# Stage 1 of a Mamba and expert-choice layer: TensorE adds the residual rows into the projection's PSUM, ScalarE evacuates, and the slots of all steps are set anew

## The reference, cut to what matters

```python
xz = einsum('bld,ed->ble', x, in_proj_w); x_, z = split(xz, 2)     # 512 + 512 features
u = silu(conv1d(x_) + b)                                           # 4 taps per feature
dt_low, B, C = split(einsum(u, x_proj_w))                          # 16 + 16 + 16
delta = softplus(dt_low @ dt_proj_w.T + dt_proj_b)
h = exp(delta * A) * h + delta * B * u                             # scan, 16 states per feature
y = einsum(h, C) + u * D_param
out = einsum('bld,ed->ble', y * silu(z), out_proj_w)               # step O
x = layernorm(x + out)                                             # the residual rows are x
```

## Time and profile before

| | us |
|---|---|
| time, median of 3 runs | 4301.18 |
| lowest and highest run | 4300.93, 4303.93 |
| the profiled execution | 4299.05 |
| its span, first to last instruction | 4297.2 |
| VectorE busy | 3740.2 |
| GpSimd busy | 3577.2 |
| TensorE busy | 3501.9 |
| ScalarE busy | 3471.5 |

### The profile page before, as it was taken

How to read it: one execution, slowest core, us unless ns; L and a number is a source line. 1 busy time by engine, 2 the same in 40 slices (tenths; PEclk the granted TensorE clock), 3 DMA queues, 4 the chain that set the end, 5 groups by cost and what they waited for, 6 DMA issues and landing times. The chain is left out here.

```text
span 4297.2 us, 57735 instructions
## 1 busy us (share of the span) xinstructions
PE 3501.9 (81%) x19574; PEld 2474.0 (58%) x19574; DVE 3740.2 (87%) x4796; ACT 3471.5 (81%) x5913; POOL 3577.2 (83%) x1887
## 2 busy tenths in 40 slices
PE   7778888888788888878888888888766399999992
PEld 3455555555555555555555555555555288989882
DVE  5899999999999999999999999999997666666665
ACT  5889999999899999999999998999885066566663
POOL 3899999999999999999999999999986256666677
PEclk9999999999999999999999999999987599999996
DMA  2667676777666676776776676676664233333346
GB/s 83 155 159 169 168 174 166 166 167 177 163 165 169 158 166 161 177 174 168 172 170 165 166 170 172 165 167 167 152 152 118 47 69 65 66 74 66 62 140 241
DMA packets 178855, 628.41 MB, mean 146 GB/s; under 512 B 33648, under 2 KB 97264, under 8 KB 119168
## 3 DMA queue, kind: packets, MB, share of 16 engines
q0 software_dynamic: 73920, 368.61, 42.7%
q1 hardware_dynamic: 104640, 256.10, 17.7%
HBM read 223.57 MB, written 68.68 MB: 68 GB/s over the span
## 5 line engine op out<-in xcount | busy, mean ns | idle before, releaser
L463 POOL TENSOR_TENSOR dbu<-du,bb 128x2048 f32<-128x2048 f32 x511 | 2434.7, 4815 | 102.8 <-DVE h L939 77.9
L939 DVE TENSOR_TENSOR_SCAN h<-da,hlast,dbu 128x512 f32<-128x512 f32 x1536 | 1868.3, 1266 | 79.7 <-POOL dbu L463 56.6
L791 PE MATMUL ht<-ident,h 128*128 128x128 f32 x8192 | 1170.1, 287 | 467.7 <-DVE h L939 183.6
L524 ACT ACTIVATE da<-dl,negA 128x512 f32<-128x512 f32 x2048 | 1413.6, 702 | 122.2 <-DVE h L939 117.0
L791 PEld LDWEIGHTS ht<-ident,h 128*128 128x128 f32 x8192 | 958.0, 146 | 882.6 <-DVE h L939 327.2
L543 ACT ACTIVATE pair<-ht,ct 128x512 f32<-128x512 f32 x896 | 591.7, 688 | 118.7 <-DMA acc<-pair 59.9
L939 DVE TENSOR_TENSOR_SCAN h<-da,dbu 128x512 f32<-128x512 f32 x512 | 592.8, 1206 | 43.6 <-POOL dbu L463 22.9
L715 PE MATMUL spare<-xin,win 128*128 128x512 f32 x1024 | 493.4, 612 | 12.2 <-DMA xin<-in_xt 7.5
L724 PE MATMUL spare<-xh,conv 128*128 128x512 f32 x1024 | 465.2, 597 | 0.9 <-ACT xh L555 0.8
L1712 ACT ACTIVATE hraw<-f,b 128x512 f32<-128x512 f32 x256 | 176.5, 689 | 223.1 <-PE f L1796 195.5
L447 POOL DMA_DIRECT2D acc<-pair x222 | 228.6, 1030 | 143.9 <-ACT pair L543 62.3
(11 more groups left out here) (244 smaller groups left out, 5724.7 us busy)
## 6 DMA issues: line engine op xcount, KB each, us to landing
acc<-pair POOLq DMA_DIRECT2D x222, 1024.0 KB, 7.2
bb<-b_rows SPq DMA_DIRECT2D x128, 1024.0 KB, 6.6
acc<-acc POOLq DMA_DIRECT2D x64, 1024.0 KB, 7.8
dl<-du POOLq DMA_DIRECT2D x62, 512.0 KB, 5.6
x_scores<-scores_and_rows SPq DMA_DIRECT2D x33, 512.0 KB, 4.5
xin<-in_xt SPq DMA_DIRECT2D x32, 512.0 KB, 4.8
sums<-scores_and_rows SPq DMA_DIRECT2D x32, 512.0 KB, 6.3
scores_and_rows<-in_x SPq DMA_DIRECT2D x31, 512.0 KB, 4.0
```

The costliest lines, as they stand in the source:

```text
L463: pool.tensor_tensor(dbu[n % 2][:], du[q][:], bb[part % 2][:, m:m + 1, :].to_broadcast([P, DT, CH]), ALU.mult).then_inc(dbu_done, 1)
L524: act.activation(da[DA_SLOT[m]][:], dl[q][:, dt, :], ACT.Exp, scale=negA[:, dt, n:n + 1]).then_inc(exp_done, 1)
L791: last = te.transpose(ht[HT_SLOT[m]][:, dt * P:(dt + 1) * P], h[n % 2][:, dt, b * P:(b + 1) * P], ident[:])
L939: dve.tensor_tensor_scan(h[n % 2][:, dt, :], da[DA_SLOT[n * DT + dt]][:], dbu[n % 2][:, dt, :], start, ALU.mult, ALU.add).then_inc(scan_do ...
```

## The change

Step O starts each 128-token block with a matmul of the identity and the residual rows, so that the bank holds the projection plus the rows; TensorE waits for the rows. ScalarE copies the bank to `xres`. VectorE's addition is removed. All tables of slots are written anew, with the same steps: of 160 lines of the diff the code and those entries stand here that the text speaks of.

```diff
-STEPS = [(0, "C", 0), (1, "C", 1), (1, "C", 2), (2, "C", 3), (2, "Y", 0), (3, "Y", 1), (4, "Y", 2), (4, "Y", 3),
-         (5, "XP", 0), (6, "T", 0), (6, "D", 0), (8, "T", 1), (8, "CT", 0), (8, "D", 1), (9, "D", 2), (9, "D", 3),
-         (9, "O", 0), (10, "L", 0), (10, "Z", 0), (11, "O", 1), (12, "Z", 1), (13, "Z", 2), (14, "Z", 3),
-         (14, "X", 0), (14, "X", 1), (15, "X", 2), (15, "X", 3)]
+STEPS = [(0, 'C', 0), (1, 'C', 1), (1, 'C', 2), (2, 'C', 3), (3, 'Y', 0), (4, 'Y', 1), (4, 'Y', 2), (4, 'Y', 3),
+ (5, 'XP', 0), (6, 'T', 0), (6, 'D', 0), (6, 'T', 1), (8, 'CT', 0), (8, 'D', 1), (8, 'D', 2), (9, 'D', 3),
+ (9, 'O', 0), (9, 'L', 0), (10, 'Z', 0), (11, 'O', 1), (12, 'Z', 1), (13, 'Z', 2), (14, 'Z', 3), (14, 'X', 0),
+ (14, 'X', 1), (15, 'X', 2), (15, 'X', 3)]
...
-ACT_AT = {(0, 0): [("X", 0), ("X", 1)], (0, 3): [("X", 2)], (1, 1): [("X", 3)], (3, 0): [("norm", 0)],
-          (3, 1): [("norm", 1), ("C", 0)], (3, 2): [("silu_z", 0)], (3, 3): [("C", 1), ("C", 2)],
-          (4, 1): [("norm", 2)], (4, 3): [("C", 3)], (6, 2): [("silu_u", 0)], (7, 1): [("norm", 3)],
...
+ (2, 3): [('silu_z', 0)],
+ (3, 0): [('C', 0)],
+ (3, 2): [('C', 1)],
+ (3, 3): [('norm', 0)],
+ (4, 1): [('norm', 1), ('C', 2)],
+ (4, 2): [('norm', 2)],
+ (5, 2): [('C', 3)],
+ (6, 2): [('norm', 3), ('silu_u', 0)],
...
+ (11, 3): [('O', 0)],
...
+ (14, 1): [('O', 1)],
...
-DVE_AT = {(4, 2): [("Y", 0)], (5, 2): [("Y", 1)], (5, 3): [("Y", 2), ("Y", 3)], (11, 2): [("O", 0)],
-          (11, 3): [("router", 0)], (13, 1): [("router", 1)], (13, 3): [("O", 1)], (15, 3): [("stats", 0)]}
+DVE_AT = {(4, 3): [('Y', 0)],
+ (5, 2): [('Y', 1)],
+ (5, 3): [('Y', 2), ('Y', 3)],
+ (11, 2): [('router', 0)],
+ (13, 1): [('router', 1)],
+ (15, 3): [('stats', 0)]}
...
-POOL_AT = {2: [("rstd", 0)], 7: [("gate", 0), ("gate", 1), ("gate", 2)], 8: [("halo", 0)], 10: [("gate", 3)],
-           12: [("delta_u", 0)], 14: [("delta_u", 1), ("scores", 0)],
-           15: [("delta_u", 2), ("delta_u", 3), ("delta_u", 4), ("delta_u", 5)]}
+POOL_AT = {3: [('rstd', 0)],
+ 5: [('gate', 0)],
+ 7: [('gate', 1), ('gate', 2)],
+ 10: [('gate', 3)],
+ 13: [('delta_u', 0), ('halo', 0)],
+ 14: [('delta_u', 1)],
+ 15: [('delta_u', 2), ('scores', 0), ('delta_u', 3), ('delta_u', 4), ('delta_u', 5)]}
...
-            (2, 0): [(0, 1)], (2, 1): [(0, 3)], (4, 0): [(2, 3)], (5, 0): [(3, 0), (3, 1), (3, 2)], (5, 1): [(3, 3)],
...
+ (4, 0): [(2, 1), (2, 3)],
+ (4, 3): [(3, 0), (3, 2)],
+ (5, 1): [(3, 1)],
...
-MAC_AT = {(0, 3): [(15, 2)], (2, 3): [(1, 0), (1, 1), (1, 2), (1, 3)], (3, 2): [(2, 0), (2, 1)], (4, 0): [(2, 2)],
-          (6, 1): [(5, 1)], (6, 2): [(5, 3)], (7, 2): [(6, 2)], (8, 1): [(7, 0)], (9, 2): [(8, 1)],
...
+MAC_AT = {(0, 3): [(15, 2)],
+ (2, 0): [(1, 0)],
+ (2, 2): [(1, 2)],
+ (3, 0): [(1, 3), (1, 1)],
+ (3, 1): [(2, 0)],
+ (4, 0): [(2, 2)],
+ (5, 1): [(4, 1)],
+ (6, 1): [(5, 1)],
+ (6, 3): [(5, 3)],
...
-BETWEEN = [0, 1, 0, 0, 0, 0, 1, 0, 1, 2, 0, 0, 0, 1, 2, 1]
+BETWEEN = [0, 1, 0, 0, 0, 0, 1, 0, 0, 1, 0, 0, 0, 0, 1, 2]
...
+            if kind == "O":
+                return x_out, 2 * k + i + 1
...
+                    if kind == "O":
+                        act.copy(xres[:, 2 * i:2 * i + 2, :].rearrange("p b f -> p (b f)"), bank[:]).then_inc(x_out, 1)
+                    elif kind == "X":
...
                         if i == 0:
                             te.wait_ge(gated, DT * (p + 1))
+                            te.sem_inc(te_passed, 1)
+                            te.wait_ge(xres_in, 16 * (p + 1))
                         for b in range(2):
+                            te.matmul(bank[:, b * 256:(b + 1) * 256], ident[:], xres[:, 2 * i + b, :],
+                                      start=True, stop=False)
                             for k in range(DT):
                                 t0 = (2 * i + b) * P
                                 last = te.matmul(bank[:, b * 256:(b + 1) * 256], g[:, k, t0:t0 + P], wo[:, k, :],
-                                                 start=k == 0, stop=k == DT - 1)
+                                                 start=False, stop=k == DT - 1)
...
-                    else:
-                        if i == 0:
-                            dve.wait_ge(xres_in, 16 * c)
-                        x = xres[:, 2 * i:2 * i + 2, :].rearrange("p b f -> p (b f)")
-                        dve.tensor_tensor(x, bank[:], x, ALU.add).then_inc(out_of[P1], 1)
```

## The result

| | before | after |
|---|---|---|
| time, median, us | 4301.06 | 4476.44 |
| lowest and highest run | 4298.23, 4303.93 | 4470.12, 4483.61 |
| the profiled execution, its span | 4299.05, 4297.2 | 4483.61, 4481.9 |
| VectorE, GpSimd busy | 3740.2, 3577.2 | 3709.2, 3573.3 |
| TensorE, ScalarE busy | 3501.9, 3471.5 | 3628.4, 3524.0 |

The account below looks back on a forecast made before the run. Bound: a loop of VectorE to the end of step 3, then GpSimd from `dbu` 5 to the next chunk. VectorE's 100.6 and GpSimd's 100.1 to 102.5 us gave 101.4, +0.7 per chunk over 31 chunks: 4322 us, range 4258 to 4358.

Parts of the forecast that it names:

- (a) to (d): Residual move: VectorE gains 1.2 us per chunk; TensorE's matmuls, ScalarE's copies and the wait for rows taken as zero.
- (a): VectorE loses two residual additions at steps 11 and 13: 1.2 us per chunk back, only if VectorE is late there.
- (b): TensorE's step O grows by 0.9 us, 1.8 per chunk; taken as zero because turns queued behind have cover.
- (e), first: the pause: `silu_z` at (2,3) takes ScalarE away 4.52 us; VectorE waits 1.4 us for `da` of (3,0).
- The estimate of 4.2: The wait for `da` at step 3 if the skill's 1.38 us drain applied, with a pause of about 7.3 us.
- (e), second: C0 behind the pause: C0's late evacuation delays C2 and its turns: VectorE waits 1.0 us, last scan of step 3 starts 1.85 later.
- the clock: Rival, chance 0.05: C2's new wait lowers TensorE's clock, up to 3.4 us per chunk; at most 4407 us.
- (e), third: `silu_u`: At (6,2) the fourth normalisation goes ahead of it; the wait for `da` of (6,3) grows from 0.68 to 1.9 us.
- GpSimd's arc: From `dbu` 5 on: scaling wait goes, gate 0 waits 0.9, `dbu` 8 comes 1.8 late; ledger 100.1 to 102.5 us.
- the 1.70 of waits for transfers: GpSimd behind `dbu` 8: this wait per chunk can go, partly or wholly, as row writes move ahead of an accumulation.
- a transfer: Rival, chance 0.15: row writes meet step 7's accumulation, step 8's waits 1.0 us; +1.7 per chunk, 4354 us.
- What would show it: Signs: `da` wait about 3.3 us, turns' wait up 1.0, `dbu` wait below 1.5, step 5's scaling wait gone.

Follow-up runs that it names:

- e1: The changed kernel with the slot tables of before, step O's copies in the slots of the old additions; 4303.61 us, 1.0012 of before.
- e5: e1 with only the fourth normalisation moved early, from (7,1) to (6,2) ahead of `silu_u`; 4393.27 us, 1.0224 of before.
- e15: The changed kernel with SyncE's read of the last quarter of B's rows waiting for `dbu` 9 instead of 7; 4416.49 us, 1.0279 of before.
- e7: The changed kernel with C0 evacuated ahead of `silu_z`, multiply-adds covering the pause, fourth normalisation back at (7,1); 4369.02 us, 1.0159 of before.
- e10: e7 with gate 0 back at step 7 instead of step 5; 4360.40 us, 1.0142 of before.
- e3: The changed kernel with `silu_z` moved back to (3,2), behind the evacuation of C1; 4475.78 us, 1.0418 of before.
- e9: e7 with ScalarE's evacuations of XP, T0 and D0 put back to (8,0), (8,1) and (8,3); 4387.89 us, 1.0199 of before.
- e11: e7 with both the evacuations of XP, T0, D0 and gate 0 put back; 4369.62 us, 1.0164 of before.
- e12: e1 with all Y steps of VectorE behind step 5 and the scalings of step 3 ahead of C3; 4353.54 us, 1.0123 of before.
- e18: e16 with the accumulations of tiles 5 and 6 a step later, at 12 and 14; 4316.67 us, 1.0040 of before.
- e8: e1 with gate 2 on VectorE at (6,2) instead of GpSimd, and router 0 at (12,0); 4332.47 us, 1.0072 of before.
- e16: The kernel before with only SyncE's read of the last quarter of B's rows waiting for `dbu` 9 instead of 7; 4284.34 us, 0.9971 of before.

## Why the prediction was wrong, point by point

The sign held; the size did not, and the range up to 4358 left the time out by 118 us.

- **(a) to (d), the residual move.** Right in sum: e1 measures +5 us for all four. The copies take 588 ns (0.59 said), TensorE doesn't wait for the residual rows, and (a)'s condition, a gain only where VectorE is the late one, decided. (b), taken at zero, looked at the turns behind step O and not at step L: in e1 the 0.9 us of a longer step O come out as the wait for the router and eat most of (a). In after nobody waits there; its tables have L a step earlier.
- **(e), first: the pause.** Right: 1.54 us of wait for `da` against 1.4, at the place named, with a pause of 4.52. The estimate of 4.2 from the Trainium skill ("ScalarE: Activation LUTs", section "What ACT_TABLE_LOAD costs") has the trace of after against it as well: the activation begins 0.01 us behind the load (1461.72).
- **(e), second: C0 behind the pause.** The mechanism was right, the term too small. C2 starts 18.27 us into the chunk (18.2 by the prediction), but was counted at 3.60 and takes 5.40 in the chunk shown, 4.7 on average; the wait for the turn is 2.1 instead of 1.0. This is the rival "the clock", which had a chance of 0.05, at 1.1 us per chunk. Step 3 ends 3.15 late, not 1.85.
- **(e), third: `silu_u`.** Right: 1.85 us on average (1.77 in the chunk shown) against 1.9.
- **GpSimd's arc.** The scaling's wait at step 5 went and gate 0 waits 0.61 (0.9 said). `dbu` 8 comes 3.35 late instead of 1.8; C2's 1.1 is the larger part of that difference.
- **The step that failed** is the sentence that behind `dbu` 8 "the 1.70 of waits for transfers can go, partly or wholly, since the row writes move ahead of the accumulation that they meet now". It moved the two row writes past the accumulation, but not the instruction queued behind them: SyncE's 1 MB read, free from the end of `dbu` 7 on, moves up as well, right ahead of the accumulation of step 7. Instead of 0 to -1.7 the arc behind `dbu` 8 measures +3.1: 3.5 more up to `dbu` 9, less 0.45 regained behind it. e5 shows it with nothing else moved (+90 us), e15 undoes it (60 us back). The rival "a transfer" had the accumulation and the waiting step right, but the wrong transfer (behind the row writes alone the accumulation lands in 7.3 us, e15) and 1.0 for it.
- **How the cases were put together.** Clock and transfer were rivals of each other and of the forecast, each with a time of its own. They lie at different places of one loop, step 3 and step 8, and both came true: 3.35 at `dbu` 8 plus 3.1 behind it are the 6.4 measured, where 1.1 to 1.8 less 0 to 1.7 were forecast. That the time lies above both rivals' times is this sum. "Three places matter" fell short as well: with both losses undone 57 to 65 us stay (e7, e10), most of it at steps 4 and 5.
- **Two loose readings.** The 0.73 us of one multiply-add are not in the earlier trace rows, which show four; the trace of before has 0.73 as the mean. The clock's 3.4 per chunk are not worked out. Neither moves the forecast.
- **What would show it.** The wait for `da` is 4.2 (3.3 said), the scaling's wait, the addition's line and the new idle time at step 3 are as said; the wait for turns grew by 1.7 (1.0 said), the excess being C2's; the wait for `dbu` was to shrink below 1.5 and grew to 4.1. That sign spoke against the sum; 1.7 of it is the transfer's, since e15 has 2.3.

## What to carry to other kernels

When a step is moved in an order written by hand, follow every queue that it releases to the next entry behind: 3.1 of the 6.4 us per chunk here came with a transfer that the change doesn't mention and that only went out earlier. Waits at different places of one loop add up, so a mishap at each place belongs into the same sum, not into rival cases. Where two engines are both within a few us of the period, a wait taken from one is worth only what the other allows: e3, e9, e11, e12 and e18 gained nothing by it. And work moved to another engine is priced by a row of that engine with the same operands, at that place: e8's gate was not.

## What the runs showed of the hardware

- A 1 MB accumulation that GpSimd issues just behind a 1 MB read of SyncE goes after it, not beside it: it lands in 12.2 us behind a read issued 0.45 us ahead of it (11.3 on average in after, 7.1 in before). The read lands in 6.6 on average against 4.7 in e16; in after it has the row writes ahead of it in its queue, the last issued 2.2 us before it in the chunk shown. The Trainium skill, "DMA: Bandwidth & Descriptors", section "Queues, rings and completion order", says that each DMA engine takes turns between the queues that have work, packet by packet. The trace shows no turns among the pieces that its rows count: 426 of SyncE's and none of GpSimd's in the 4.8 us behind the issue. Whether such a piece is a packet in the page's sense, no run here shows.
- TensorE's clock fell behind idle times of 2.52 us (0.72 over C2) and of 2.06 and 0.92 us (0.55 over the turns and Y1), both inside a stretch where the engine is otherwise granted 1.00. It doesn't fall each time: the gap of 2.52 us stands in all 25 chunks of after and the clock falls over C2 in 15 of them; gaps of 1.48 and 0.92 us bring it down over the turns and Y1 in 9 of 25 (e10). What follows the gap pays: eight fp32 matmuls of C2 5.40 instead of 3.60, eight transposes 1.97 instead of 1.06.
- A 128x512 fp32 product of two SBUF tiles on VectorE took 3.2 us on average (e8) while GpSimd ran the same product on other tiles; VectorE's products with one operand in PSUM took 0.73.
